# Dummy matmuls on TensorE in the nine normalisations of a four-layer transformer kernel

## The reference

```python
def _layernorm(x, axis=-1, eps=1e-05):
    m = jnp.mean(x, axis=axis, keepdims=True)
    v = jnp.var(x, axis=axis, keepdims=True)
    return (x - m) / jnp.sqrt(v + eps)
...
    x = x + _L0_xattn_ref(_layernorm(x, axis=-1), ctx_1024, ctx_1024, ...)
    x = x + _L0_ffn_ref(_layernorm(x, axis=-1), ...)
    x = x + _L1_xattn_ref(_layernorm(x, axis=-1), ctx_1024, ctx_1024, ...)
    x = x + _L1_ffn_ref(_layernorm(x, axis=-1), ...)
    x = x + _L2_xattn_ref(_layernorm(x, axis=-1), ctx_1024, ...)
    x = x + _L2_ffn_ref(_layernorm(x, axis=-1), ...)
    x = x + _L3_xattn_ref(_layernorm(x, axis=-1), ctx_1024, ...)
    x = x + _L3_ffn_ref(_layernorm(x, axis=-1), ...)
```

## The kernel before, in words

| call | what it normalises | router | stage behind it |
|---|---|---|---|
| n0 | x, tiles arriving by DMA | no | context transposes, then `project_small` p0, `attend_small` |
| n1 | x, two scales at once, second result x2 | no | `project_self`, `attend_self` |
| n3 | x2, root mean square | 4 experts | `experts_mixed` e0 |
| n4 | x | no | `project_wide` p1, `attend_wide` |
| n5 | x | 8 experts | `experts_sorted` |
| n6 | x | no | `project_small` p2, `attend_small` |
| n7 | x, result also in two parts | 8 experts | `experts_gated` |
| n8 | x | no | `attend_two_way` |
| n9 | x, result also in two parts | 64 experts | `experts_many` |

## Time and profile before

### The profile page before, as it was taken

How to read it: one execution, slowest core, us unless ns; L and a number is a source line. 1 busy time by engine, 2 the same in 40 slices (tenths; PEclk the granted TensorE clock), 3 DMA queues, 4 the chain that set the end, 5 groups by cost and what they waited for, 6 DMA issues and landing times. The chain is left out here.

```text
span 1596.8 us, 24399 instructions
## 1 busy us (share of the span) xinstructions
PE 1283.8 (80%) x7148; PEld 1032.2 (65%) x7148; DVE 1024.7 (64%) x2047; ACT 734.5 (46%) x1260; POOL 620.8 (39%) x598
## 2 busy tenths in 40 slices
PE   4896669997997899721997499699946659999997
PEld 2673459987664599720886267588833438787875
DVE  3885678887324276660665466677768767667675
ACT  2443446665332554430654254455523325455553
POOL 1311634431000133245233131389844116676665
PEclk9996779999898899955999599699976669999998
DMA  3500011110000000131111100133202025343333
GB/s 89 143 0 1 0 41 36 39 39 5 1 0 0 20 1 0 60 112 55 35 48 32 44 1 0 45 97 97 95 19 103 1 60 125 109 130 115 126 115 104
DMA packets 69931, 85.64 MB, mean 54 GB/s; under 512 B 14282, under 2 KB 40269, under 8 KB 69850
## 3 DMA queue, kind: packets, MB, share of 16 engines
q1 hardware_dynamic: 67250, 79.94, 17.3%
q0 software_dynamic: 2272, 4.24, 0.8%
q10 hardware_dynamic: 336, 0.59, 0.2%
HBM read 69.98 MB, written 8.92 MB: 49 GB/s over the span
## 5 line engine op out<-in xcount | busy, mean ns | idle before, releaser
L2356 POOL TENSOR_TENSOR e_h<-e_h,e_gate 128x512 f32<-128x512 f32 x128 | 187.8, 1484 | 145.8 <-DVE e_h L2408 89.9
L2413 DVE TENSOR_TENSOR e_h_low<-e_h,e_h_high 128x512 fp32r<-128x512 f32 x132 | 117.8, 893 | 75.6 <-ACT e_h_high L2343 75.4
L2343 ACT ACTIVATE e_h_high<-e_h 128x512 fp32r<-128x512 f32 x132 | 83.5, 633 | 97.8 <-POOL e_h L2356 90.1
L228 PE MATMUL n_ps_t<-ident,n_zn 128*128 128x128 f32 x128 | 34.4, 433 | 90.5 <-DVE n_zn L167 82.7
L2408 DVE TENSOR_TENSOR e_h<-e_s,e_ps_b 128x512 f32<-128x512 f32 x132 | 89.4, 678 | 13.1 <-ACT e_s L2328 8.7
L1001 PE MATMUL u_ps_o<-u_vaug,u_pT 128*128 128x72 f32 x768 | 96.9, 269 | 0.0
L1001 PEld LDWEIGHTS u_ps_o<-u_vaug,u_pT 128*128 128x128 f32 x768 | 93.3, 192 | 0.0
L2328 ACT ACTIVATE e_s<-e_ps_a 128x512 f32<-128x512 f32 x132 | 77.7, 589 | 31.5 <-PE e_ps_a L1364 28.4
L228 PEld LDWEIGHTS n_ps_t<-ident,n_zn 128*128 128x128 f32 x128 | 23.9, 224 | 98.2 <-DVE n_zn L167 78.3
L932 POOL TENSOR_TENSOR u_kbd<-u_keys,groupmask 96x512 fp32r<-96x512 f32 x60 | 62.8, 1067 | 62.4 <-DMA u_keys<-s_k 37.2
L1028 ACT ACTIVATE u_sm<-u_sm 128x512 f32<-128x512 f32 x96 | 60.6, 631 | 54.5 <-DVE u_sm L1060 53.9
(11 more groups left out here) (439 smaller groups left out, 3901.3 us busy)
## 6 DMA issues: line engine op xcount, KB each, us to landing
e_gate<-gates_by_expert SPq DMA_DIRECT2D x256, 128.0 KB, 3.0
e_gate<-gates_by_expert SPq DMA_DIRECT2D x32, 256.0 KB, 3.4
w_raw<-in_L1w SPq DMA_DIRECT2D x24, 256.0 KB, 4.2
u_qs<-s_q SPq DMA_DIRECT2D x16, 192.0 KB, 2.6
u_keys<-s_k SPq DMA_DIRECT2D x8, 384.0 KB, 3.5
w_w<-in_L2w SPq DMA_DIRECT2D x24, 128.0 KB, 2.7
sorted<-blank SPq DMA_DIRECT2D x1, 2535.0 KB, 17.6
e_zb<-sorted SPq DMA_DIRECT2D x13, 195.0 KB, 2.5
```

The costliest lines, as they stand in the source:

```text
L2343: nc.scalar.activation(h_parts[k % 3][0][:, :], h[k % 3][:, :], ACT.Copy).then_inc(high_ready, 1)
L2356: nc.gpsimd.tensor_tensor(h[c % 3][:, :], h[c % 3][:, :], gate[pair % SLOTS][:, :], ALU.mult)\
L2413: nc.vector.tensor_tensor(h_parts[k % 3][1][:, :], h[k % 3][:, :], h_parts[k % 3][0][:, :], ALU.subtract).then_inc(low_ready, 1)
```

## The change

A helper `keep_busy` issues matmuls of the 128x128 all-ones matrix in two-byte precision, `ones_b`, with itself repeated four times, 512 columns each, into a PSUM bank of its own that nobody reads. PE issues 36 of them at the start of each of the nine normalisations, behind the wait for the identity matrix (which only n0 has) and ahead of the wait for the first group of zn, and 4 more ahead of the wait for each of the other three groups: 48 in each, 432 in all, each with its load of weights. They wait for nothing, and nothing but PE's own queue waits for them. `ones_b` is there before: `experts_sorted` uses it, and it is written by DVE (`memset`) in the program's first block.

```diff
+def keep_busy(nc, bank, ones, times):
+    for _ in range(times):
+        nc.tensor.matmul(bank[:, :].rearrange("p (a c) -> p a c", c=P), ones,
+                         ones.unsqueeze(1).broadcast_to([P, 4, P]), start=True, stop=True)
+
 def normalise(nc, tag, src, ident, root, out_T, center=True, second=None, out_natural=None, channel_scale=1.0,
               gate_w=None, logits=None, arrived=None, ident_loaded=None, then=None, loads=None, parts=None,
-              meanwhile=None, before=None, rows=None):
+              meanwhile=None, before=None, rows=None, ones=None):
...
         ps_t = [m.ps(f"ps_t{i}") for i in range(2)]
+        spare = m.ps("spare")
...
             if ident_loaded is not None:
                 pe.wait_ge(ident_loaded, 16)
+            keep_busy(nc, spare, ones, 36)
             for g in range(GROUPS):
+                if 0 < g:
+                    keep_busy(nc, spare, ones, 4)
                 pe.wait_ge(normed, g + 1)
                 if g >= 2:
                     pe.wait_ge(evacuated, g - 1)
...
-        normalise(nc, "n4_", x, idn, root_ln, zT, then=ACT.Exp)
+        normalise(nc, "n4_", x, idn, root_ln, zT, then=ACT.Exp, ones=ones_b[:, :])
```

More of the change, by code:

```diff
@@ L2563, in build @@
         normalise(nc, "n0_", x, idn, root_ln, zT, arrived=x_loaded, ident_loaded=ident_loaded, then=ACT.Exp,
-                  loads=load(first, first_loaded))
+                  loads=load(first, first_loaded), ones=ones_b[:, :])
         with ExitStack() as stack:
@@ L2608, in build @@
             normalise(nc, "n1_", x, idn, root_both, zT, second=root_ln, out_natural=x2,
-                      channel_scale=self_w["n1"][:, 0:1])
+                      channel_scale=self_w["n1"][:, 0:1], ones=ones_b[:, :])
             with ExitStack() as inner:
@@ L2617, in build @@
             normalise(nc, "n3_", x2, idn, root_rms, zT, center=False, channel_scale=self_w["n2"][:, 0:1],
-                      gate_w=self_w["gate"], logits=logits[4], then=ACT.Exp)
+                      gate_w=self_w["gate"], logits=logits[4], then=ACT.Exp, ones=ones_b[:, :])
             experts_mixed(nc, "e0_", x, x2, self_w, zT, logits[4], rank)
         clear_spent(nc)
-        normalise(nc, "n4_", x, idn, root_ln, zT, then=ACT.Exp)
+        normalise(nc, "n4_", x, idn, root_ln, zT, then=ACT.Exp, ones=ones_b[:, :])
         with ExitStack() as stack:
@@ L2634, in build @@
             normalise(nc, "n5_", x, idn, root_ln, zT, gate_w=gate1, logits=logits[8], then=ACT.Exp,
-                      loads=weights.first_loads, rows=rows[0])
+                      loads=weights.first_loads, rows=rows[0], ones=ones_b[:, :])
             experts_sorted(nc, "e1_", x, logits[8], rank, sort, weights, idn, rows, drams[0],
@@ L2638, in build @@
         clear_spent(nc)
-        normalise(nc, "n6_", x, idn, root_ln, zT, then=ACT.Exp)
+        normalise(nc, "n6_", x, idn, root_ln, zT, then=ACT.Exp, ones=ones_b[:, :])
         with ExitStack() as stack:
@@ L2651, in build @@
             normalise(nc, "n7_", x, idn, root_ln, zT, gate_w=gate2, logits=logits[8], then=ACT.Exp, parts=z,
-                      loads=weights.first_loads, meanwhile=weights.first_splits)
+                      loads=weights.first_loads, meanwhile=weights.first_splits, ones=ones_b[:, :])
             experts_gated(nc, "e2_", x, z, logits[8], rank, weights, idn, gates_dram, zT,
@@ L2656, in build @@
         many.make_room(m)
-        normalise(nc, "n8_", x, idn, root_ln, zT, then=ACT.Exp, before=lambda act: many.make_high(act, 0))
+        normalise(nc, "n8_", x, idn, root_ln, zT, then=ACT.Exp, before=lambda act: many.make_high(act, 0), ones=ones_b[:, :])
         attend_two_way(nc, "t3_", x, two_way, zT, ctxT, ctx_nat, idn, ones[:, :], many)
@@ L2660, in build @@
         logits[64] = m.sb("logits64", [P, TILES, 64])
-        normalise(nc, "n9_", x, idn, root_ln, zT, gate_w=gate3, logits=logits[64], then=ACT.Sigmoid, parts=z)
+        normalise(nc, "n9_", x, idn, root_ln, zT, gate_w=gate3, logits=logits[64], then=ACT.Sigmoid, parts=z, ones=ones_b[:, :])
         experts_many(nc, "e3_", x, z, logits[64], bias3[:, :], many, idn,
```

## The result

The changed kernel takes 1608.51 us (median of 19 runs, 1592.32 to 1612.06), the kernel before in the same session 1597.70 us (19 runs, 1593.31 to 1601.84). The ratio is 1.0052, 95% interval 1.0031 to 1.0073: slower by about 8 us, with 5 to 12 in the interval; the two medians alone lie 10.8 us apart. The forecast was 1606, range 1594 to 1619.

The account below looks back on a forecast made before the run. DVE's statistics bound the waits for first transposes, PE at half clock the router groups and projection starts. Lateness 18.1 less 7.6 in groups and 3.3 in next stages gave +7.2 us: 1606 us, range 1594 to 1619.

Parts of the forecast that it names:

- 10.2 started low, 7.9 started high: Ahead of each normalisation's first transposes: 36 dummies take 10.2 us from a low clock, 7.9 us from a high one.
- 18.1 us lost: Waits for the first transposes: dummies outlast PE's idle time, making the nine normalisations 18.1 us late in sum.
- the one-in-three case: n3's first transposes: 2.9 us late if the clock has fallen, 0.6 if it stays up; 1.3 taken.
- Gained: 1.7 + 1.6 + 1.7 + 2.6: Groups of the router normalisations n5, n3, n7 and n9: higher clock shortens transposes and routers, 7.6 us gained.
- I cost this at nothing: Groups in normalisations without router: four dummies between, 0.9 us at high clock, offset by shorter transposes; no net cost.
- What the next stage gets: 0.9 each for p1 and p2, 1.0 for project_self, 0.5 for e0: Stages behind the normalisations: a clock left high by the dummies may shorten their starts, 3.3 us gained in all.
- the holding rival: Clock stays high through each gap to the next stage; p1 gains 2.5 us, sum -2.6, 1596 us; chance 0.20.
- if p1 starts high: Sign of being wrong: the projections p1, behind n4, begin at high clock after PE's 2.49 us idle gap.
- though never longer than today: Next stages: if the clock falls in the gap, the stage starts low, but for no longer than before the change.
- Low at every next stage: Rival: clock low at every normalisation's start and again at every next stage; +19 us, 1618 us; chance 0.20.
- The dummies do not raise the clock: Rival: all-ones two-byte dummies are too little work; 36 take 15.5 us each time, 1710 us; chance 0.03.

Follow-up runs that it names:

- the run with 72: 72 dummies ahead in place of 36 in each normalisation, four between kept, against the changed kernel: 1666.46 us, ratio to the kernel before 1.0425.
- the run with the plain ones alone: The changed kernel with all dummies only in the five normalisations without a router (n0, n1, n4, n6, n8): 1613.64 us, 1.0080 to the kernel before.
- 36 and 0: The changed kernel with 36 dummies ahead and none between the groups, in all nine normalisations: 1598.37 us, 1.0004 to the kernel before.
- both sized runs: Changed kernel with 20 ahead in n0, 26 in n7, 18 elsewhere; four between in n4, n6, n7, n9 only; with attend_self dummies 1587.14 us, without 1586.02.

## Why the prediction was right, and where it was not

**The price of a dummy and the rise (right).** "10.2 started low, 7.9 started high": 9.2 to 10.4 and 7.5 to 7.8 measured. The 0.22 is confirmed by the run with 72: 69.9 / (9 x 36) = 0.216.

**"18.1 us lost" (right, 17.7).** By place: n0 2.4 for 2.1, n1 3.2 less the 0.5 that its rest gives back for 2.8, n4 3.4 for 3.3, n5 1.0 and n9 1.3 for 1.2. n3 (2.2 for 1.3) was the one-in-three case, a low start. n6 (2.3 for 3.3) had risen sooner and n8 (1.3 for 2.5) had started high in this profile; in the run with the plain ones alone they were 3.4 and 2.9. Which level the first dummy meets differs from run to run, so that the sum came closer than its places is luck: n3 is over by 0.9, n6 and n8 under by 2.2.

**"Gained: 1.7 + 1.6 + 1.7 + 2.6" (right in kind, 9.5 in size with 7.6 forecast).** n5 2.3, n3 2.2, n7 2.3, n9 2.7. The sizes of the terms were a little high: n5's sum took 0.5 for a group's transposes and 0.9 for its four dummies and for its router, and from start to start they measured 0.44, 0.86 and 0.82. "I cost this at nothing" for plain groups was right for the change as it stands, as -1.0 for the clock and +1.0 for the dummies between, which the run with none between parted.

**"What the next stage gets: 0.9 each for p1 and p2, 1.0 for project_self, 0.5 for e0" (the step that failed).** p1 gave 2.45 in each of the eight profiles with the four in n4: the holding rival's figure, and "if p1 starts high" was among the signs of being wrong. Without the four it gave nothing. project_self gave 1.5 for 1.0. p2 took 8.15 us for 9.18, but so it did in two runs without dummies in n6; where the clock held through it (three profiles) it took 6.50. e0 gave nothing here, 1.5 in two other runs. And the attention behind project_self cost 9.2 us, the slow spell, a term that the sum does not have. I had taken it that a stage could start low "though never longer than today" and that any continuous stream lifts the clock within 3 to 5.5 us. The attention's loop at half clock is continuous, 23.32 of 24 us, and stayed at 0.51. Together: -3.3 forecast, +5.6 measured in the profile, 2.0 of it in n8's stage and within what untouched stages differ by.

**The sum.** +7.2 forecast; +8 by the ratio (5 to 12), +10.8 by the medians, +13.4 between the profiles. Against the profile it is 6 us short: 8.7 at n1's stage and 2 at n8's upwards, 2 in the groups and 1.5 at p1 downwards. The median is nearer, presumably since the spell is not in every run (five of 19 took 1592 to 1600). With the attention's start kept busy, the same dummies cost nothing (0.9988, 0.9965 to 1.0012), where the forecast's terms would have it +7.2. So the number is right in part by luck: a spell of 9.2 us in most runs, which nobody had forecast, stands against gains some 4 us larger than forecast, and stages that differ by the run make up the rest. The verdict holds, the mechanism of the loss half so: lateness, as forecast, plus a spell that wasn't.

**The rivals.** "The clock holds" was true at p1 only with the four between. "Low at every next stage" was true of p1 without them. "The dummies do not raise the clock" is out. On transposes I had set the trace against a rule; at n4, 36 and 0 leave transposes alone with 2.35 us of work in 5.98, and p1 starts low. That agrees with the Trainium skill, "TensorE: Matmul & The Clock Gate", "Part 4: PE-mode transpose", and equally with the plain fact of PE being idle for most of that time; no run here parts the two, and the earlier trace rows still stand against it: the clock rose at 194.5 us, when PE had run nothing but transposes since 186.5.

**What stays open.** Why the spell comes. It does not need dummies in n0 (n1 alone had it). The profiles with 72 and with none ahead did not have it, but one profile without it proves little, as runs of one kernel fall on either side. One thing parts the profiles, in the clock's record. In the four with the spell the clock fell 6.3 to 6.6 us before the attention's first matmul and stayed low for 34 us; in the eight without it (the attention's start as it was) it fell 8.3 to 15.6 us before, and rose 17 to 24 us after its fall. That the moment of the fall against the attention's ramp settles it fits all twelve; nothing moved that moment alone, so it is argued, not shown.

## What to carry to other kernels

Dummies ahead of a wait are free only up to the idle time at the price of the low clock: count the idle time, divide by the low-clock duration (0.43 us here), and stop. Here 18, with the four between, did for the clock what 36 did at eight of the nine places and cost 18 us less. The count has a lower end too: where 18 ended some 3 us before the transposes, the clock fell in some profiles and held in others (n5: it fell in both sized runs and held with 18 everywhere). A few dummies between the groups are what carries the clock over the gap to the next stage; put them where a long stage at low clock follows or the groups are sparse, and leave them out where the transposes follow closely on dummies. After such a change read the granted clock of all later stages, not only of those changed: a loop that PE bounds takes nearly twice as long per step at half clock (3.23 us for 1.70), and can stay there though PE is never idle. And profile more than one execution where the runs of a kernel fall into groups.

## What the runs showed of the hardware that I had not expected

- **A busy PE can stay at 1.2 GHz for over 20 us.** The low stretch is 34.1 us long; PE has 2.47 us of work in its first 10.6, and then is busy for 23.32 of 24 us at 0.51 in the changed kernel. With 18 ahead this row, 117 matmuls in 24 us, none idle (the clock rises at 233.1):

```profile
212.00:236.00 24.00, 24.00 (x117) 21.50 (x116) 12.22 (x20) 10.69 (x18) 6.11 (x6) 0.56 0.09 25
236.00:245.00 9.00, 9.00 (x72) 7.85 (x71) 6.98 (x12) 6.14 (x10) 2.56 (x4) 1.00 0.09 25
```

  The Trainium skill, "TensorE: Matmul & The Clock Gate", Part 1 (on the clock gate), has it that activity releases the low clock; by the busy time that a trace records, this loop disagrees. Most of its matmuls stream 72 or 128 columns behind a weight load each, as the routers' 8 do, which also stay at 0.50 while busy for 10.29 of 10.93 us.
- **One kernel's runs can fall into groups**, without any change in it: 1589 to 1597 and 1603 to 1606 us with dummies in n1 alone; the kernel before, in the same session, went from 1592.7 to 1608.5.
- **The clock held over p1's gap of 2.50 us** when the groups ahead were filled, and fell when they held transposes alone; the gap was the same.
